# Attention, mLSTM and mixture-of-experts in one kernel: clears of DRAM regions moved to steps 1 to 9, small units in other banks, VectorE's and ScalarE's work in another order

## What is computed

```python
x = _layernorm(x + attn(x, Wq, Wkv, Wo, bo))          # 16 heads of 64, softmax over 128 keys
x = _layernorm(x + mlstm(x, ctx, ctx, igate, fgate, rms_scale))
x = _layernorm(x + ffn(x, gamma, beta, Wr, br, W1, b1, W2, b2))
# mlstm: 4 heads; gates from concat(q, k, v); log_d = cumsum(log f) differences + i, lower triangle;
#        d = exp(log_d - max); c = q k^T / 8 * d; h = c / (max(sum c, exp(-m)) + eps) v; rms norm of each head
# ffn:   xn = layernorm(x); probs = softmax(xn @ Wr + br); the best 2 of 8 experts for each token;
#        expert e: relu(xn @ W1[e] + b1[e]) @ W2[e] + b2[e], weighted by probs, plus a term of the biases
```

## Time and profile before

| | us |
|---|---|
| median of 3 runs (lowest, highest) | 877.47 (872.62, 878.78) |
| the profiled execution | 873.39 |
| its span, first to last instruction | 871.6 |
| PE busy, DVE busy | 709.3, 467.3 |
| ACT busy, POOL busy | 328.4, 246.4 |
| loop over pairs | about 25 to 454 |
| drain | about 454 to 530 |
| experts | about 530 to 800 |

### The profile page before, as it was taken

How to read it: one execution, slowest core, us unless ns; L and a number is a source line. 1 busy time by engine, 2 the same in 40 slices (tenths; PEclk the granted TensorE clock), 3 DMA queues, 4 the chain that set the end, 5 groups by cost and what they waited for, 6 DMA issues and landing times.

```text
span 871.6 us, 14654 instructions
## 1 busy us (share of the span) xinstructions
PE 709.3 (81%) x4812; PEld 604.3 (69%) x4813; DVE 467.3 (54%) x1078; ACT 328.4 (38%) x987; POOL 246.4 (28%) x196
## 2 busy tenths in 40 slices
PE   5798989988088988989858415999999999998763
PEld 4687877878077868778656314888888888787421
DVE  4334454843255846558465773555555555555345
ACT  4475666746055746646443201222222222222111
POOL 3100010300311302113034347637227300600473
PEclk9899999989589989899785556999999999999755
DMA  9533333331301001010052015615324411110243
GB/s 312 150 116 115 128 116 116 127 115 37 126 14 37 26 19 55 1 38 25 2 181 66 7 42 175 188 61 164 130 66 156 138 36 42 61 37 19 68 122 113
DMA packets 62507, 77.36 MB, mean 89 GB/s; under 512 B 5836, under 2 KB 54520, under 8 KB 62456
## 3 DMA queue, kind: packets, MB, share of 16 engines
q1 hardware_dynamic: 53832, 47.29, 16.9%
q0 software_dynamic: 8608, 29.37, 10.3%
q10 hardware_dynamic: 16, 0.01, 0.0%
HBM read 45.04 MB, written 31.62 MB: 88 GB/s over the span
## 4 chain that ended last, share of the span: by engine, by line
PE 62%; DVE 11%; ACT 11%; POOL 7%; issue 5%; DMA 4%; POOLq 0%; SPq 0%; DVEq 0%; ACTq 0%
PE bank L919 13%; PE bank L693 7%; PE bank L695 6%; PE bank L694 6%; ACT arena L1026 6%; PE bank L889 4%; PE bank L891 4%; PE bank L890 4%; PE bank L899 4%; POOL arena L683 4%; PE bank L838 3%; PE bank L807 3%; DVE arena L1187 2%; PE bank L771 2%; ACT arena L999 1%
## 5 line engine op out<-in xcount | busy, mean ns | idle before, releaser
L919 PE MATMUL bank<-w_ring,hidT_hi 128*128 x320 | 119.9, 408 | 3.3 <-DVE hidT_lo L1535 3.3
L1026 ACT ACTIVATE arena<-bank,negmx 128x128 f32<-128x128 f32 x256 | 90.7, 373 | 51.7 <-DVE negmx L1179 51.5
L1142 ACT ACTIVATE hidT_hi<-bank 128x512 fp32r<-128x512 f32 x80 | 43.5, 596 | 174.6 <-PE bank L899 174.6
L618 POOL DMA_INDIRECT xg_dram<-arena,slot x32 | 34.2, 1067 | 174.8 <-DVE slot L1378 112.0
L919 PE MATMUL bank<-w_ring,hidT_lo 128*128 x320 | 83.4, 281 | 0.0
L1508 DVE TENSOR_TENSOR arena<-bank,b_rep 128x512 f32<-128x512 f32 x80 | 55.3, 691 | 41.9 <-PE bank L891 41.5
L1185 DVE RECIPROCAL rinv<-rsum 128x8 f32<-128x8 f32 x32 | 6.5, 203 | 127.4 <-ACT arena L1026 127.4
L889 PE MATMUL bank<-w_ring,xgT_hi 128*128 x160 | 67.8, 424 | 4.5 <-DVE xgT_lo L1527 2.7
L919 PEld LDWEIGHTS bank<-w_ring,hidT_hi 128*128 128x128 f32 x320 | 60.1, 188 | 15.0 <-issue 4.0
L1514 DVE TENSOR_REDUCE work<-bank 128x256 f32<-128x512 f32 x40 | 27.7, 691 | 79.5 <-PE bank L919 79.5
L574 POOL TENSOR_TENSOR w_ring<-w_raw,w_ring 128x2048 fp32r<-128x2048 f32 x14 | 64.4, 4597 | 1.2
(11 more groups left out here) (240 smaller groups left out, 1839.7 us busy)
## 6 DMA issues: line engine op xcount, KB each, us to landing
xg_dram<-zeros SPq DMA_DIRECT2D x9, 2176.0 KB, 9.1
w_raw<-in_L_ffn_W_dram POOLq DMA_DIRECT2D x16, 1024.0 KB, 5.8
work<-xg_dram SPq DMA_DIRECT2D x40, 128.0 KB, 2.0
y_dram<-work SPq DMA_DIRECT2D x40, 128.0 KB, 1.7
b_rep<-in_L_ffn_b_dram POOLq DMA_DIRECT2D x8, 512.0 KB, 4.1
work<-gmax_dram SPq DMA_DIRECT2D x14, 256.0 KB, 3.7
arena<-in_x_dram SPq DMA_DIRECT2D x8, 256.0 KB, 2.8
xres<-in_x_dram SPq DMA_DIRECT2D x1, 2048.0 KB, 15.1
```

The source lines that it names most:

```text
L919: last = pe.matmul(o, l, r, start=c == 0 and l is both[0], stop=c == FC - 1 and l is both[0])
L1026: last = nc.scalar.activation(probs[:, n % 2, h * S:(h + 1) * S], ps_score[:, h * S:(h + 1) * S], ACT.Exp, bias=negmx[:, n % 2, h:h + 1], ...
```

## The change

- SP's nine `clear_rows` are issued in steps 1 to 9 (pair 0 step 1 to pair 2 step 1), one in each.
- T's products go to banks 4 and 5 (those of the transposed weights) in the loop, L, R and G to bank 7 (that of the output projection), each in a time in which the bank rests; PE gets the waits that this needs. The ring of two banks has x, q, k, v, X, C, N, S and U.
- In the table: T first in step 1, G ahead of v there; R from step 2's first part to its second; S from the end of step 3 to its second place.
- DVE: `weigh` ahead of `logits_in`; `choose`, `gate_sums` and `head_sums` ahead of `weights_of`; `find_slots` behind it.
- ACT: `soft_gates` at the head of step 2, `exp_of_m` at its end.
- Drain: POOL loads b1's first row ahead of the weights, later ones later, and takes `rstd_of_pair` first; ACT rounds expert 0's weights ahead of N's copy, and expert 1's too; DVE does the rests of expert 0 and half of expert 1 between the chain's pieces, POOL the other half after the last scatter.

```diff
-        ps_ring = bank[0:6]
+        ps_ring = [*bank[0:6], bank[7]]
...
             if s == 1:
-                return (of("L", i - 3) + of("X", i - 1) + of("x", i + 1) + of("v", i, 1, 0) + of("T", i - 2),
-                        of("v", i, 0, 1) + of("v", i, 1, 1) + of("G", i - 1))
+                return (of("T", i - 2) + of("L", i - 3) + of("X", i - 1) + of("x", i + 1) + of("v", i, 1, 0),
+                        of("G", i - 1) + of("v", i, 0, 1) + of("v", i, 1, 1))
             if s == 2:
-                return (of("U", i - 2, 0) + of("R", i - 3) + of("q", i + 1, 0) + of("U", i - 2, 1) + of("k", i + 1, 0),
-                        of("q", i + 1, 1) + of("k", i + 1, 1))
-            return (of("v", i + 1, 0, 0) + of("w", i, 0, 0) + of("q", i + 1, 2),
-                    of("w", i, 0, 1) + of("k", i + 1, 2) + of("S", i - 1))
+                return (of("U", i - 2, 0) + of("q", i + 1, 0) + of("U", i - 2, 1) + of("k", i + 1, 0),
+                        of("q", i + 1, 1) + of("R", i - 3) + of("k", i + 1, 1))
+            return (of("v", i + 1, 0, 0) + of("S", i - 1) + of("q", i + 1, 2) + of("w", i, 0, 0),
+                    of("w", i, 0, 1) + of("k", i + 1, 2))
...
-                    place[un] = []
-                    for _ in range(2 if un[0] in "TB" else 1):
-                        k = turn % banks_of
-                        turn += 1
-                        place[un].append((k, uses[k]))
+                    if not at_end and un[0] in "TLRG":
+                        ks = (4, 5) if un[0] == "T" else (6,)
+                    else:
+                        ks = [(turn + k) % (6 if at_end else 2) for k in range(2 if un[0] in "TB" else 1)]
+                        turn += len(ks)
+                    place[un] = [(k, uses[k]) for k in ks]
+                    for k in ks:
                         uses[k] += 1
...
-                    if s < 2 and 2 * i + s <= E:
-                        done(sp, ("q", i, 3) if s == 0 else ("v", i, 1, 1))
-                        clear_rows(2 * i + s)
+                    if 1 <= STEPS * i + s <= E + 1:
+                        done(sp, {0: ("q", i, 3), 1: ("v", i, 1, 1), 2: ("k", i + 1, 1), 3: ("k", i + 1, 2)}[s])
+                        clear_rows(STEPS * i + s - 1)
...
+            def load_after_first(part):
 
                 pool.wait_ge(w_split, part + 1)
                 load_raw(1, part)
+
+            def rest_of_second():
+
+                both = w_ring[:, 1, W_WORDS:2 * W_WORDS].rearrange("p (g k n) -> p g k n", k=2, n=D)
+                pool.wait_ge(w_rounded, 4)
+                pool.tensor_tensor(both[:, :, 1, :], w_raw[:, KC * F:2 * KC * F].rearrange("p (g n) -> p g n", n=D),
+                                   both[:, :, 0, :].bitcast(F32), ALU.subtract).then_inc(w_split, 1)
+                pool.wait_ge(w_split, 4)
+                for part in range(2):
+                    load_raw(2, part)
...
                     if (i, s) == (Z, 2):
                         done(pool, ("v", Z, 1, 1))
+                        load_bias(0)
                         for part in range(2):
                             load_raw(0, part)
-                        load_bias(0)
-            load_bias(1)
             scale_xn(A)
+            rstd_of_pair(Z)
             for b in range(2):
                 mask(Y, b)
-            rstd_of_pair(Z)
-            load_bias(2)
+            load_bias(1)
             scatter(A)
             head_norm(Y)
+            load_after_first(0)
             for b in range(2):
                 mask(Z, b)
             both_norms(Y)
             scale_xn(Y)
+            load_after_first(1)
             head_norm(Z)
             both_norms(Z)
+            load_bias(2)
             scatter(Y)
             scatter(Z)
+            rest_of_second()
             for part in range(2):
-                split_first(part)
-            for e in range(1, RING):
-                for part in range(2):
-                    split(e, part)
+                split(2, part)
...
                     pe.wait_ge(gws_ready, 1)
+                    if p < Z:
+                        pe.wait_ge(wo_read, 2 * (p + 1))
...
                 elif kind == "T":
+                    if p < Y:
+                        pe.wait_ge(pT_copied, STEPS * (p + 2) + 1)
...
                     read(pe, ("N", p))
+                    if p < A:
+                        pe.wait_ge(wo_read, 2 * (p + 3))
...
+                if half == 0 and b == 0:
+                    for un in (("G", i - 1), ("R", i - 3)):
+                        if un in place:
+                            read(pe, un)
...
+                if n % STEPS == 1 and n // STEPS >= 2:
+                    read(pe, ("T", n // STEPS - 2))
...
+                    if s == 2 and i >= 1:
+                        soft_gates(i - 1)
                     copies(before[:early])
                     if n + 1 < STEPS * PAIRS:
                         exponentials(n + 1, 0)
                     copies(before[early:])
                     if s == 0 and i >= 2:
                         decays(i - 2, 1)
-                    if s == 3 and i >= 1:
-                        exp_of_m(i - 1)
                     act.wait_ge(pT_done, n + 1)
                     nc.scalar.copy(pT, ps_pT).then_inc(pT_copied, 1)
                     copies(after[:1])
...
                         exponentials(n + 1, 1)
                     if s == 1 and i >= 3:
                         choice_exp(i - 3)
+                    copies(after[1:])
                     if s == 2 and i >= 1:
-                        soft_gates(i - 1)
-                    copies(after[1:])
+                        exp_of_m(i - 1)
                     act.wait_ge(oT_done, n + 1)
                     nc.scalar.copy(oT_hi[:, b, 4 * half:4 * half + 4, :],
                                    ps_oT.rearrange("p (c t) -> p c t", c=4)).then_inc(oT_rounded, 1)
             for b in range(2):
                 decays(Y, b)
             copy_unit(("C", Z))
-            copy_unit(("N", A))
             act.wait_ge(wo_done, B)
             for part in range(2):
-                round_first(part)
+                round_early(0, part)
+            copy_unit(("N", A))
...
                 copy_unit(("U", Z, b))
             copy_unit(("N", Y))
             choice_exp(Y)
+            for part in range(2):
+                round_early(1, part)
             copy_unit(("N", Z))
...
+            def rest_early(e, part):
+
+                n = (512, D)[part]
+                both = w_ring[:, e, part * W_WORDS:(part + 1) * W_WORDS].rearrange("p (g k n) -> p g k n", k=2, n=n)
+                dve.wait_ge(w_rounded, 2 * e + part + 1)
+                dve.tensor_tensor(both[:, :, 1, :], w_raw[:, part * KC * F:(part + 1) * KC * F]
+                                  .rearrange("p (g n) -> p g n", n=n), both[:, :, 0, :].bitcast(F32), ALU.subtract)\
+                    .then_inc(w_split, 1)
...
+                    if s == 1 and i >= 2:
+                        weigh(i - 2)
                     if s == 1 and i >= 3:
                         logits_in(i - 3)
                     if s == 1 and i + 1 < PAIRS:
                         rest_x(i + 1)
-                    if s == 1 and i >= 2:
-                        weigh(i - 2)
-                    if s == 2 and i >= 3:
-                        find_slots(i - 3)
+                    if s == 1 and i >= 3:
+                        choose(i - 3)
+                    if s == 2 and i >= 1:
+                        gate_sums(i - 1)
+                    if s == 2 and i >= 2:
+                        head_sums(i - 2)
                     if s == 3 and i >= 2:
                         add_heads(i - 2)
                     if n + 1 < STEPS * PAIRS:
                         weights_of(n + 1)
                     if s == 0 and i >= 1:
                         normalise(i - 1)
-                    if s == 1 and i >= 3:
-                        choose(i - 3)
                     if s == 1 and i >= 1:
                         read_gates(i - 1)
-                    if s == 2 and i >= 1:
-                        gate_sums(i - 1)
-                    if s == 2 and i >= 2:
-                        head_sums(i - 2)
+                    if s == 2 and i >= 3:
+                        find_slots(i - 3)
...
             weigh(Y)
+            rest_early(0, 0)
             logits_in(A)
...
             both_norms(Y)
+            rest_early(0, 1)
             head_sums(Z)
...
             both_norms(Z)
+            rest_early(1, 0)
             logits_in(Z)
```

22 lines of the change are left out of this document (7 added, 15 removed).

## The result

| | before | after |
|---|---|---|
| median of 4 runs each on one chip (lowest, highest) | 875.05 (872.42, 878.78) | 844.41 (844.13, 845.75) |
| the profiled execution | 873.39 | 844.13 |

What follows compares the result with a forecast made beforehand. PE was taken as nearly full except for a 21.8 us slice where POOL waits for zeros, short waits per pair and the drain. Terms 22.5 + 7.2 + 3 + 1 + 2.8 + 4.3 = 40.8 off 873.4 gave 833 us, range 816 to 850.

Steps and rivals of the forecast that it cites:

- The hole: Slice of 21.8 us without PE in pair 3, POOL waiting for zeros; earlier clears take 22.5 us off.
- a clear in the way of the maxima: Rival: in pair 2 a clear delays the store and reload of maxima, 8 us; 841 us, chance 0.06.
- The loop's order, pairs 3 to 6: Loop: each pair takes 52.6 us instead of 54.4, 1.8 off, times four pairs: 7.2 us.
- 3.8 us earlier: Pair 5, step 1: waits of 1.09 and 0.77 and 1.2 of slow clock go, so step 2's scores start 3.8 us earlier.
- k's stretch at the low clock: Step 2 behind U's wait: 12 matmuls of 0.21 instead of 0.12 us, costing 1.1 us.
- G stands ahead of the v units now: Step 1: v's copy then holds ACT's second half of the exponentials; no size given.
- Pairs 1 and 2: Early loop, without `choose` and R: pair 1 gets 1 us shorter, pair 2 gets 3 us shorter.
- Drain: Between loop and experts: 2.8 us off at the loop's end and drain's head, 4.3 off at the drain's tail.
- the stretched issue: Drain: the moved VectorE rests will stretch a scatter of pair 6 instead, where POOL has 8 us to spare.
- The loop gives nothing: Rival: U's wait and the later `head_norm` take all 7 us, the drain's clock its 3; 843 us, chance 0.14.
- The later `head_norm`: Step 3: it queues behind POOL's four scatters, DVE waits some 5 us in `add_heads`, covered by PE's other work.
- Slower: Rival: longer idle in step 2 leaves PE at half clock until the pair's end; 883 to 923 us, chance 0.02.

Runs made afterwards that it cites:

- the clears alone: The kernel before the change with one edit, the nine clears issued in steps 1 to 9 of the loop: 848.9 us, ratio 0.9728.
- its own run: The changed kernel with G put back behind the two v units in step 1: 825.3 us, ratio 0.9492.
- the old lists: The changed kernel with VectorE's and ScalarE's lists of the loop, and S's place, as before the change: 844.1 us, ratio 0.9681.
- clears and drain: The kernel with the change's clears and drain edits, but the loop's order, banks and lists as before the change: 841.6 us, ratio 0.9641.
- `choose` behind the gates: The changed kernel with `choose` moved from ahead of `weights_of` to behind `read_gates` in step 1: 842.8 us, ratio 0.9692.
- choice_exp early: The changed kernel with `choice_exp` of step 1 moved on ScalarE ahead of the copy pT: 816.3 us, ratio 0.9365.

## Why the prediction was right or wrong

- **The whole.** The time lies in the range, but not because each term was right: the hole and the drain carry 21.7 and 7.3 of the profile's 29.3 us, and the loop's terms (7.2 us, and 4 more for pairs 1 and 2) came out at nothing. It is the time of the rival that had 0.14.
- **The hole (22.5 us).** Right: 21.7 in the profile, and 54.5 us for pair 3 in the clears alone. The clears cost nothing where they lie now. The rival of a clear in the way of the maxima fell with pairs 1 and 2 at 44.0 and 48.9 us.
- **The loop's order, pairs 3 to 6 (7.2 us).** Wrong: against the 54.4 us a pair that the forecast set, these four take 389.09 - 171.16 = 217.9 us, 0.3 more than 4 x 54.4. The steps of the chain were nearly right, counted from the scores of step 0: step 2's scores at 22.7 us (forecast 22.1), gates read at 28.5 (28.1), U at 30.6 (30.1), k at 32.6 (32.3). Three terms were mis-sized. "3.8 us earlier" for step 2's scores was 3.2 (15.73 to 12.49 us for step 1 of pair 5), and the terms that the forecast names for it (1.09, 0.77 and 1.2) add up to 3.1 only. "k's stretch at the low clock" (1.1 us) was 2.6, since the transposes and q run slowly too; step 3's scores came at 42.1 instead of 40.4. Step 3 took 12.47 us where it took 11.54 in pair 5 before, 0.9 more, and the forecast had 0.4.
- **G ahead of v.** "G stands ahead of the v units now" was written down and given no price. It makes v's copy, the exponentials, `choice_exp`, `choose` and both chains behind them 2.0 us later. By its own run that is 14 us in all, more than the whole gain that the loop's order was to bring. The forecast followed the chain with this delay in it, and never asked what the chain would be without it.
- **The larger error was one of reading.** The forecast followed the chain choose, weights, gates, U and gave it its right times. It did not ask what the removed waits are worth while this chain sets the step. The earlier trace rows had the hint: VectorE idle 3.16 us for the exponentials just ahead of the weights, with `choose` still to be done behind them and inside the chain. The trace of after has it in full, 6.43 us of idle time for a `choice_exp` whose input had been ready. The move of `choose` ahead of `weights_of` without `choice_exp` took it out of neither chain: before the change it stood ahead of the gates and of the next maxima as well, and with the old lists the wait is 5.2 us for q's copy.
- **The pair that was followed.** In the profile before, step 1 of pair 5 took 15.73 us, but 14.7 in pairs 3 and 4, and 14.7 in all four pairs of the clears alone. The wait of 1.09 us stands there in all of them, but the low clock behind it, for which the forecast had 1.2 us, only in the profile before and only from pair 5 on. Against the kernel with the clears alone the new step 1 gains 2.2 us, not 3.8.
- **Pairs 1 and 2 (1 and 3 us).** Wrong in sign: 0.3 and 0.9 us longer. Pair 2's step 1 is 1.6 us shorter. Step 2 gives back 1.6 (waits of 0.36 for U and 0.93 for q's copy, clock 0.97 over the pair, before 1.00). Step 3 takes 12.47 us where it took 11.53: S's products and the wait of 1.15 us for the exponentials were on PE's path, and the forecast had priced S only in the pairs behind. In pair 1 this eats the 1.0 us that step 2 gains.
- **Drain (2.8 and 4.3 us).** Right in its rows: the bias wait is gone, the last scatter and the row load have the forecast times, and the stretched issue went to pair 6 beside a VectorE rest, as the step said. The sum, 7.3 against 7.1, agrees partly by luck. From pair 7's marker to the first row load it takes 115.2 us before and 111.3 in the clears alone, whose drain is the old one, so 3.9 of the 7.3 are not the drain's edits; 2.7 of them lie in step 1 of pair 7 (16.49 and 13.81 us), where the wait is the same and the granted clock is 0.52 in one and 1.00 in the other; why it differs stays open. The drain's own edits are the step from there to clears and drain: 4.4 us up to the row load and 2.1 behind it.
- **Which rival came.** "The loop gives nothing", 843 us, at 0.14. Its time was right. Of its causes the wait for U was there (4.19 us), but freed alone it is worth nothing (`choose` behind the gates, 842.8 us): the wait moves to q's copy. The later `head_norm` is covered up to pair 7, and the drain came out with its forecast sum.
- **Slower.** The clock came back within the step, 1.00 from 365 us on, and did not stay low to the pair's end.

## What to carry to other kernels

When an edit removes several short waits of the bound engine, find first the one chain that releases the step's last wait, and ask whether the edit shortens it. If it doesn't, the waits only merge, and the merged wait costs more than its length, because the clock falls behind it. An idle stretch of another engine that ends on a tiny operation queued behind a long one (here 6.4 us of VectorE for a `choice_exp` of 0.2 us) is the place to look: moving that one instruction was worth 25 us, and 9 of these are edits that had shown nothing without it. And a place in a queue that is written down without a price is a term like any other: here the place of one unit of PE ahead of another cost 14 us by the ratios.

## What the runs showed of the hardware

- Idle time of 4.19 and 0.85 us on PE was followed by a granted clock of 0.66 over 10 us (between the levels of 1.2 and 2.4 GHz), in which k's products start 0.21 us apart instead of 0.12, and cost 2.6 us beyond the wait. The 5 us around the end of a wait of 2.97 us had 0.66, and waits of 0.49 and 0.86 us were followed by 1.00.
- The length of a wait alone does not tell. PE has the same wait of 1.09 us in step 1 of pair 7 in the kernel before (to 414.94) and in the one with the clears alone (to 393.84). The low clock followed the first and not the second; what decides was not shown:

```profile
415.00:420.00 5.00, 4.23 (x20) 0.52 0.00 0
```

```profile
394.00:399.00 5.00, 4.23 (x33) 1.00 0.00 0
```

- Products whose result is thrown away, put into the wait, kept the clock at 1.00 and made the kernel about 6 us faster by the ratios, 10 by the profiles, though it does more work.
- The stretched issue of an indirect transfer follows VectorE's long subtraction: 2.64 us at 481.05 beside one of 2.29 us that began at 480.55, where its neighbours take 0.97 to 1.09. Clears and drain has the same pair of rows (2.65 us at 479.41, 478.92), and choice_exp early too (2.65 at 454.36, 453.87).
